# In the last rounds of the token stage, the stores of normed rows and h go ahead of the outputs' stores

## The chip, the core and the metric

The kernel runs on one core of one Trainium2 chip. A core has a matrix engine (TensorE, in the profile PE, its weight loads PEld), VectorE (DVE), ScalarE (ACT), GpSimd (POOL) and SyncE (SP), which here only issues DMAs. Each engine runs its own list of instructions in order and waits on semaphores for the others. The metric is the device time of one execution in microseconds (us).

## The reference

The reference takes x, 8192 tokens (4 sequences of 2048) of 512 numbers, through one transformer layer:

```python
xn = layernorm(x)
cq, ckv = xn @ Wc + bc, xn @ Wckv + bckv
q = [cq @ Wcq + bcq, cq @ Wqr + bqr]      # per token: 16 heads x (32 + 16)
k = [ckv @ Wck + bck, xn @ Wkr + bkr]
v = ckv @ Wv + bv                         # 16 heads x 32
attn = softmax(q k^T / sqrt(48))          # between the heads of one token
x1 = x + layernorm((attn v) @ Wo + bo)
xf = layernorm(x1)
scores = softmax(xf @ gate_w.T)           # 64 experts, the best 6 of each token
routed = sum over them of score * down_e(silu(gate_e(xf)) * up_e(xf))
shared = (silu(xf @ Wsg.T) * (xf @ Wsu.T)) @ Wsd.T
out = x1 + layernorm(routed + shared)
```

The attention runs over the 16 heads of one token, not over tokens. In the reference 16 of each head's 48 numbers of q and k are also turned by an angle of the token's position (rotary embedding). Scores are taken between heads of the same token only, so both sides turn alike and the scores don't change; the kernel leaves the turning out. `h` below is the hidden product silu(gate) * up of the shared part.

## The kernel before

Two programs run one behind the other. The **token stage** (`token_pipeline`) goes over 64 tiles of 128 tokens. The **expert stage** (`experts_and_norm`) gathers each expert's rows from device memory, multiplies, adds them to accumulators in device memory, and then a last pass adds the shared part and norms. Between the two stands a barrier of all engines.

The token stage is a software pipeline. Every engine has a function `iteration(i, par)`; in round i it works on several tiles at once: tile i+1 is normed, i projected, i-1 gets its q, k and v, i-2 its attention, i-3 its output product, i-4 its x1 and second norm, i-5 its gate, up and routing scores, and i-6 is stored. Rounds -2 to 7 and 62 to 69 are unrolled with plain numbers, the rest is a loop over registers. `active(t)` is true in the loop, and for a plain number where 0 <= t < 64.

The attention's output `o` has its heads in the partitions and must be turned into rows of tokens. This goes over device memory: DVE writes `o` in round i-1 (L867, counted by `d_pv`), SP stores it with four DMAs in round i (L368, counted by `o_out`), waits until they have landed, and loads it back with four more as `oin` (L383, `o_in`). PE transposes `oin` (L557) ahead of the second half of the gate and up product and of the product with Wo; in PE's order these come before the transposes of prob and the product of prob with v (L598), which makes the next `o`. The stores' rows in device memory are 128 bytes long.

In the same round SP stores the finished tile i-6: `xf` (L372, 288 KB: normed rows and routing scores, waits for `d_r`, the last DVE instruction of round i-1, L882) and `h` (L375, 192 KB, waits for `d_h`). These stand between the stores of `o` and their reload. `xf` has two buffers; DVE norms tile i-4 into one (L799, in the profile L732 of the helper `normalise`) once the store of tile i-6 has landed (`xf_out`). The order of the DMAs on SP is written out by hand; all of SP's DMAs go through one hardware queue.

At the end of rounds 65 and 66 ScalarE issues the weights of the first four experts (L690 to L694: each time two experts of 768 + 384 KB), right behind its copy of the ranks. In rounds 66 and 67 SP also loads the ranks for the expert stage.

Of the kernel before, what the change touches and what calls it, by code (L numbers as in the profile page):

```python
# [41 lines left out]
NT = T // P  # L42
# [60 lines left out]
def settle(eng):  # L103

    eng.nop(nofuse=True)
# [47 lines left out]
def token_pipeline(nc, x, cst, w_lat, b_lat, w_q, b_q, w_ck, b_ck, w_v, b_v, w_o, b_o, w_gu,  # L153
                   x1_d, xf_d, h_d, acc_d, v_d, o_d, rank_d, wlat, wq, wck, wv, load_expert, c, tri, all_ranks, ranks_in):
    ctx = ExitStack()
    with ctx:
        def sb(name, shape, dt=F32):
            return ctx.enter_context(nc.sbuf_tensor(name, shape, dt))
# [4 lines left out]
        def count(name, per=1, n=1, place=0):  # L163
            return Count(sem(name), per, NT, n, place)
# [41 lines left out]
        xf = sb("xf", [P, 2, D + E])  # L206
        xfT = sb("xfT", [P, 2, KD, P], F32R)
        th = sb("th", [P, SI])
        h = sb("h", [P, 2, SI])
# [56 lines left out]
        h_out = [count(f"h_out{n}", 16, 2, n) for n in range(2)]  # L266
        acc_out = count("acc_out", 32)
        xf_out = [count(f"xf_out{n}", 16, 2, n) for n in range(2)]
# [43 lines left out]
        d_h = count("d_h", 4)  # L312
        d_r = count("d_r", 8)
# [14 lines left out]
        def active(t):  # L328
            return not isinstance(t, int) or 0 <= t < NT

        def pipeline(eng, iteration):
            for i in range(FIRST, LOOP):
                iteration(i, i % 2)
            with eng.Fori(0, PAIRS) as r:
                for u in range(2):
                    iteration(r * 2 + (LOOP + u), (LOOP + u) % 2)
            for i in range(REST, LAST):
                iteration(i, i % 2)

        def rows(ap, t):  # L340
            return ap[t * P:(t + 1) * P, :] if isinstance(t, int) else ap[bass.ts(t, P), :]


        @block.sync
        def _(sp):
            for t in range(2):
                sp.dma_start(xin[:, t, :], rows(x, t)).then_inc(x_in[t].sem, 16)
            sp.dma_start(c[:], cst).then_inc(consts_in, 16)
            for n, (stage, _, _, src) in enumerate(parts):
                if n in SPLIT_BEFORE:  # L350
                    sp.wait_ge(part_lo, SPLIT_BEFORE[n])
                sp.dma_start(stage, src).then_inc(part_in[n], 16)
                if n == KD - 1:
                    sp.dma_start(blat[:], b_lat.partition_broadcast(P)).then_inc(latent_bias_in, 16)

            def load_ranks(a, b):
                sp.dma_start(all_ranks[a:b].rearrange("n e t -> n (e t)"),
                             rank_d[a:b].rearrange("n e t -> n (e t)")).then_inc(ranks_in, 16)

            def iteration(i, par):  # L360
                if active(i - 3):
                    sp.wait_ge(d_pv.sem, d_pv.at(i - 3))
                    sp.wait_ge(o_in.sem, o_in.at(i - 5))
                    dst = o_d[1 - par].rearrange("(c g b) (x d) -> g b x c d", c=8, g=2, b=2, d=DH)
                    src = o[:].rearrange("p (c b d) -> p b c d", c=8, b=2)
                    for g in range(2):
                        for b in range(2):
                            sp.dma_start(dst[g, b], src[64 * g:64 * g + 64, b]).then_inc(o_out.sem, 16)  # L368
                if active(i - 6):
                    sp.wait_ge(d_r.sem, d_r.at(i - 6))  # L370
                    settle(sp)
                    sp.dma_start(rows(xf_d, i - 6), xf[:, par, :]).then_inc(xf_out[par].sem, 16)  # L372
                    sp.wait_ge(d_h.sem, d_h.at(i - 6))
                    settle(sp)
                    sp.dma_start(rows(h_d, i - 6), h[:, par]).then_inc(h_out[par].sem, 16)  # L375
                if active(i - 3):
                    sp.wait_ge(o_out.sem, o_out.at(i - 3))
                    settle(sp)
                    sp.wait_ge(pe_oT.sem, pe_oT.at(i - 4))
                    settle(sp)  # L380
                    src = o_d[1 - par].rearrange("c (h t d) -> t c h d", t=B4, d=DH)
                    for n in range(B4):
                        sp.dma_start(oin[n:P:B4, :].rearrange("p (h d) -> p h d", d=DH), src[n]).then_inc(o_in.sem, 16)  # L383
                if active(i + 2) and (not isinstance(i, int) or i >= 0):

                    sp.wait_ge(d_ln[0].sem, d_ln[0].at(i))
                    settle(sp)
                    sp.dma_start(xin[:, par, :], rows(x, i + 2)).then_inc(x_in[par].sem, 16)
                if isinstance(i, int) and i == FIRST:
                    sp.wait_ge(zeroed, 2)  # L390
                    sp.dma_start(xf_d[T:T + CAP, :], zero[:]).then_inc(scratch_init, 16)
                    for a in acc_d:
                        sp.dma_start(a[T:T + CAP, :], zero[:, 0:D]).then_inc(scratch_init, 16)
                if active(i - 4):
                    sp.wait_ge(g_x1.sem, g_x1.at(i - 4))
                    settle(sp)
                    sp.dma_start(rows(x1_d, i - 4), x1[:]).then_inc(x1_out.sem, 16)
                if active(i - 3):
                    sp.wait_ge(g_x1.sem, g_x1.at(i - 4))
                    settle(sp)  # L400
                    sp.dma_start(xres[:], rows(x, i - 3)).then_inc(xres_in.sem, 16)
                if active(i - 5):
                    for a in acc_d:
                        sp.dma_start(rows(a, i - 5), zero[:, 0:D]).then_inc(acc_out.sem, 16)
                if active(i - 6):
                    sp.wait_ge(a_rank.sem, a_rank.at(i - 6))
                    settle(sp)
                    if isinstance(i, int) and i - 6 >= NT - DIRECT:
                        dst = all_ranks[i - 6:i - 5]
                    else:  # L410
                        dst = rank_d[i - 6] if isinstance(i, int) else rank_d[bass.ds(i - 6, 1)].rearrange("o e t -> (o e) t")
                    sp.dma_start(dst, rank[:, par, :]).then_inc(rank_out[par].sem, 16)
                if isinstance(i, int) and i == 1:
                    sp.wait_ge(zeroed, 3)
                if active(i - 1):
                    sp.wait_ge(d_v.sem, d_v.at(i - 1))
                    sp.wait_ge(v_in[1 - par].sem, v_in[1 - par].at(i - 3))
                    sp.dma_start(v_d[1 - par], v[:]).then_inc(v_out.sem, 16)
                    sp.wait_ge(v_out.sem, v_out.at(i - 1))
                    settle(sp)  # L420
                    sp.wait_ge(pe_pv.sem, pe_pv.at(i - 3))
                    settle(sp)
                    src = v_d[1 - par].rearrange("(cg b t) (j d) -> b (t j) cg d", cg=NBLK, b=2, j=H)
                    for b in range(2):
                        sp.dma_start(vbd[64 * b:64 * b + 64, 1 - par, :, b, :], src[b]).then_inc(v_in[1 - par].sem, 16)
                if isinstance(i, int) and i == NT + 2:
                    for n in range(2):
                        sp.wait_ge(rank_out[n].sem, rank_out[n].at(NT - 18 + n))
                    load_ranks(0, NT - 16)
                if isinstance(i, int) and i == NT + 3:  # L430
                    for n in range(2):
                        sp.wait_ge(rank_out[n].sem, rank_out[n].at(NT - DIRECT - 2 + n))
                    load_ranks(NT - 16, NT - DIRECT)

            pipeline(sp, iteration)
            for n in range(2):
                sp.wait_ge(rank_out[n].sem, rank_out[n].at(NT - 2 + n))
            sp.wait_ge(acc_out.sem, acc_out.at(NT - 1))
            sp.wait_ge(x1_out.sem, x1_out.at(NT - 1))
            for n in range(2):  # L440
                sp.wait_ge(h_out[n].sem, h_out[n].at(NT - 2 + n))
                sp.wait_ge(xf_out[n].sem, xf_out[n].at(NT - 2 + n))
            sp.wait_ge(scratch_init, 48)
# [163 lines left out]
        def _(act):  # L607

            def split(i):

                for n, (stage, w, m, _) in enumerate(parts):
                    if PART_AT[n] == i:
                        act.wait_ge(part_in[n], 16)
                        nc.scalar.copy(w[:, 0, m, :], stage).then_inc(part_hi, 1)
# [799 lines left out]
```

## Time and profile before

| | us |
|---|---|
| median of 3 runs | 1982.51 |
| lowest and highest | 1980.75, 1984.57 |
| profiled execution | 1972.49 |
| its span, first to last instruction | 1970.5 |
| PE busy | 1813.3 (92%) |
| DVE busy | 1482.7 (75%) |
| ACT busy | 1039.2 (53%) |
| POOL busy | 554.7 (28%) |

All times inside the span are microseconds from its start. The token stage ends at about 1357. A row of an engine's order of time gives start, duration, engine (with q where its sequencer issues a DMA), line, operation, destination and source; in brackets stands how long the engine had been idle before it, and what ended this. The names of buffers stand without numbers: `bank` is any of the PSUM banks. A helper's line stands for all its calls.

### The profile page before, as it was taken

Reading aid. Unit: us, or ns where it says so; the run is one execution under the profiler, and the core shown is the slowest. Engines: PE = TensorE matmul, PEld = TensorE weight load, DVE = VectorE, ACT = ScalarE, POOL = GpSimd, SP = SyncE. Lnnn points to the kernel's source line nnn. Section 1 sums busy time; section 2 is a strip of 40 time slices with the busy share of each in tenths; the row PEclk is TensorE's granted clock in tenths of the full one; section 3 lists DMA queues with packets and bytes.
Section 4 is the critical chain, followed back from the end, with each engine's and each line's share of the span. In section 5 each row is a group of like instructions: output and inputs, shape, how many; then the busy total and the mean of one; then the engine's idle time right before and its main releaser. Section 6 shows DMA issues by size and latency. Waiting matters only on the chain. (4 is left out here: it accounts for less than half of the span.)

```text
span 1970.5 us, 49884 instructions
## 1 busy us (share of the span) xinstructions
PE 1813.3 (92%) x14529; PEld 1439.2 (73%) x14529; DVE 1482.7 (75%) x3871; ACT 1039.2 (53%) x2257; POOL 554.7 (28%) x773
## 2 busy tenths in 40 slices
PE   5899999999999999999999999865799999978886
PEld 4788888888888888888888888754455555546564
DVE  6688888888888888888888888854354445439897
ACT  4666666666667676666666666631233333323333
POOL 1112111111212121212121212111344444427777
PEclk8899999999999999999999999987899999989999
DMA  5355656555555555555555555566999999979994
GB/s 194 77 155 132 157 129 158 131 148 142 140 151 141 150 138 153 136 154 136 154 136 153 137 154 133 144 155 202 307 309 312 306 308 310 291 210 398 396 397 163
DMA packets 540056, 384.01 MB, mean 195 GB/s; under 512 B 423848, under 2 KB 432168, under 8 KB 539944
## 3 DMA queue, kind: packets, MB, share of 16 engines
q1 hardware_dynamic: 519456, 324.99, 56.9%
q0 software_dynamic: 14336, 35.66, 7.9%
q10 hardware_dynamic: 6208, 22.68, 3.0%
q8 instruction: 27, 0.44, 0.1%
q14 instruction: 29, 0.24, 0.0%
HBM read 232.46 MB, written 150.63 MB: 194 GB/s over the span
## 5 line engine op out<-in xcount | busy, mean ns | idle before, releaser
L617 ACT COPY kT<-bank 48x256 f32<-48x256 f32 x512 | 309.0, 604 | 12.6
L895 POOL TENSOR_SCALAR ve<-mv 128x1 f32<-128x1 f32 x192 | 42.4, 221 | 959.8 <-DVE mv L728 959.8
L1103 PE MATMUL e_gu<-w,xgT 128*128 128x384 f32 x512 | 187.2, 510 | 13.9 <-issue 12.9
L617 ACT COPY qT<-bank 48x256 f32<-48x256 f32 x512 | 188.1, 367 | 13.3 <-PE bank L453 2.3
L460 PE MATMUL bank<-wgu,xfT 128*128 128x416 f32 x512 | 187.6, 366 | 4.3 <-ACT xfT L617 3.8
L461 PE MATMUL bank<-wgu,xfT 128*128 128x416 f32 x512 | 181.8, 355 | 0.0
L1264 DVE SCALAR_TENSOR_TENSOR tanh<-tanh,e_gu 128x192 f32<-128x192 f32 x64 | 22.6, 354 | 167.9 <-ACT tanh L1190 167.9
L1103 PEld LDWEIGHTS e_gu<-w,xgT 128*128 128x128 f32 x512 | 94.2, 194 | 72.4 <-issue 18.8
L1347 POOL DMA_INDIRECT acc_scratch<-eo,sidx x64 | 101.5, 1586 | 123.7 <-ACT eo L1186 107.5
L1126 PE MATMUL e_ps<-w,hidT 96*128 96x512 f32 x256 | 127.6, 621 | 1.6 <-ACT hidT L1178 0.9
L464 PE MATMUL bank<-wgu,xfT 128*128 128x416 f32 x512 | 119.2, 355 | 0.3 <-DVE xfT L737 0.3
L897 POOL TENSOR_TENSOR rstd<-ve,mhalf 128x1 f32<-128x1 f32 x192 | 114.5, 596 | 16.0
L913 POOL TENSOR_TENSOR x<-yn,xres 128x512 f32<-128x512 f32 x64 | 82.2, 1284 | 116.1 <-DVE yn L732 116.1
L489 PE MATMUL bank<-wlat,xT 128*128 128x512 f32 x256 | 108.2, 423 | 1.4 <-issue 1.4
L746 DVE SCALAR_TENSOR_TENSOR th<-th,bank 128x176 f32<-128x176 f32 (+1 forms) x128 | 44.9, 351 | 85.3 <-ACT th L655 82.3
L1178 ACT COPY hidT<-e_ps 96x256 f32<-96x256 f32 x64 | 23.6, 368 | 159.4 <-PE e_ps L1110 159.4
L1376 POOL TENSOR_TENSOR f_res<-f_acc,f_res 128x512 f32<-128x512 f32 x64 | 95.1, 1508 | 33.5 <-ACT f_acc L1207 17.8
L1207 ACT ACTIVATE f_acc<-f_acc,f_shift,f_rstd 128x512 f32<-128x512 f32 x64 | 48.7, 808 | 105.8 <-POOL f_shift L1368 105.8
L460 PE MATMUL bank<-wo,oT 128*128 128x512 f32 x256 | 102.5, 400 | 1.4 <-ACT oT L617 1.4
L480 PEld LDWEIGHTS score_ps<-kT,qT 48*64 48x64 f32 x4096 | 69.2, 138 | 46.7 <-issue 46.7
L617 ACT CAST oT<-bank 128x512 fp32r<-128x512 f32 x64 | 37.6, 587 | 124.5 <-PE bank L453 124.5
L490 PE MATMUL bank<-wlat,xT 128*128 128x512 f32 x256 | 102.8, 402 | 0.0
(178 smaller groups left out, 4884.8 us busy)
## 6 DMA issues: line engine op xcount, KB each, us to landing
w<-w_eg SPq DMA_DIRECT2D x60, 768.0 KB, 6.0
acc_scratch<-zero SPq DMA_DIRECT2D x130, 256.0 KB, 4.1
w<-w_ed SPq DMA_DIRECT2D x60, 384.0 KB, 7.6
xf_scratch<-xf SPq DMA_DIRECT2D x64, 288.0 KB, 2.1
xin<-x SPq DMA_DIRECT2D x64, 256.0 KB, 3.0
v_scratch<-v SPq DMA_DIRECT2D x64, 256.0 KB, 3.7
vbd<-v_scratch SPq DMA_DIRECT2D x128, 128.0 KB, 3.3
o_scratch<-o SPq DMA_DIRECT2D x256, 64.0 KB, 2.3
```

The lines of the kernel that those rows point to most:

```text
L460: nc.tensor.matmul(dst, a[:, 0], b[:, 0], start=(n == 0), stop=False)
L461: nc.tensor.matmul(dst, a[:, 0], b[:, 1], start=False, stop=False)
L464: last = nc.tensor.matmul(dst, a[:, 1], b[:, 0], start=False, stop=(n == len(lhs) - 1))
L489: nc.tensor.matmul(dst, a[:, 0], b[:, 0], start=(n == 0), stop=False)
L490: nc.tensor.matmul(dst, a[:, 0], b[:, 1], start=False, stop=False)
L617: nc.scalar.copy(dst, src).then_inc(done.sem, 1)
L897: nc.gpsimd.tensor_tensor(rstd[n][:], ve[n][:], mhalf[:], ALU.pow).then_inc(g_rstd[n].sem, 1)
L913: nc.gpsimd.tensor_tensor(x1[:], yn[:], xres[:], ALU.add).then_inc(g_x1.sem, 1)
L1103: last = nc.tensor.matmul(gu_ps[par], xgT[:, par, n, :], w1[:, place, n, :], start=(n == 0), stop=(n == KD - 1))
L1126: last = nc.tensor.matmul(out_ps, hidT[:, n, :], w2[0:PI, (place - 1) % NW, n, :], start=(n == 0), stop=(n == 1))
L1347: nc.gpsimd.indirect_dma_start(acc_d[1 - par], bass.IndirectOffsetOnAxis(sidx[:, (place - 1) % NW, :].bitcast(U32), 0), eo[:, (place - 1) ...
L1376: nc.gpsimd.tensor_tensor(r, acc[:, u, n * D:(n + 1) * D], r, ALU.add).then_inc(g_sum.sem, 1)
```

## The change

SP's stores of `xf` and `h` are put in a function of their own, `store_rows`. In rounds with a plain number i of 64 or more it is called ahead of the stores of `o`; in all others it is called behind them, as before. In rounds 67 to 69 there are no stores of `o`. No other engine's program is changed.

```diff
+            def store_rows(i, par):
+                if active(i - 6):
+                    sp.wait_ge(d_r.sem, d_r.at(i - 6))
+                    settle(sp)
+                    sp.dma_start(rows(xf_d, i - 6), xf[:, par, :]).then_inc(xf_out[par].sem, 16)
+                    sp.wait_ge(d_h.sem, d_h.at(i - 6))
+                    settle(sp)
+                    sp.dma_start(rows(h_d, i - 6), h[:, par]).then_inc(h_out[par].sem, 16)
+
             def iteration(i, par):
+                if isinstance(i, int) and i >= NT:
+                    store_rows(i, par)
                 if active(i - 3):
                     sp.wait_ge(d_pv.sem, d_pv.at(i - 3))
                     sp.wait_ge(o_in.sem, o_in.at(i - 5))
...
                             sp.dma_start(dst[g, b], src[64 * g:64 * g + 64, b]).then_inc(o_out.sem, 16)
-                if active(i - 6):
-                    sp.wait_ge(d_r.sem, d_r.at(i - 6))
-                    settle(sp)
-                    sp.dma_start(rows(xf_d, i - 6), xf[:, par, :]).then_inc(xf_out[par].sem, 16)
-                    sp.wait_ge(d_h.sem, d_h.at(i - 6))
-                    settle(sp)
-                    sp.dma_start(rows(h_d, i - 6), h[:, par]).then_inc(h_out[par].sem, 16)
+                if not isinstance(i, int) or i < NT:
+                    store_rows(i, par)
                 if active(i - 3):
                     sp.wait_ge(o_out.sem, o_out.at(i - 3))
```

## Rows read from the trace of the kernel before

**Rows 1.** the page's share of busy time: engine, busy us (share), instructions.
```profile
...
PE 1813.3 (92%) x14529; PEld 1439.2 (73%) x14529; DVE 1482.7 (75%) x3871; ACT 1039.2 (53%) x2257; POOL 554.7 (28%) x773
...
```

**Rows 2.** rounds as windows: us, engines' busy us (instructions), clock, DMA, GB/s.
```profile
...
1246.46:1266.58 20.12, 19.67 (x198) 17.21 (x196) 17.00 (x41) 13.22 (x30) 2.84 (x5) 1.00 0.50 131
1266.58:1286.18 19.60, 15.63 (x173) 13.83 (x173) 15.43 (x37) 11.52 (x27) 2.82 (x5) 1.00 0.52 135
...
1306.94:1333.80 26.86, 13.37 (x53) 11.31 (x53) 10.14 (x26) 3.01 (x8) 4.11 (x6) 0.73 0.87 229
...
```

**Rows 3.** SP's order of time, 1262 to 1330: start us, us, instruction.
```profile
...
1266.58 2.63 SPq L368 DMA_DIRECT2D o_scratch<-o  x4
1269.30 0.57 SPq L372 DMA_DIRECT2D xf_scratch<-xf  x1
...
1270.87 3.58 SPq L383 DMA_DIRECT2D oin<-o_scratch  x4
...
1286.18 2.63 SPq L368 DMA_DIRECT2D o_scratch<-o  x4
...
1290.47 2.58 SPq L383 DMA_DIRECT2D oin<-o_scratch  x4
...
1306.94 4.34 SPq L368 DMA_DIRECT2D o_scratch<-o  x4
1311.38 3.18 SPq L372 DMA_DIRECT2D xf_scratch<-xf  x1
1314.65 0.38 SPq L375 DMA_DIRECT2D h_scratch<-h  x1
1316.35 2.59 SPq L383 DMA_DIRECT2D oin<-o_scratch  x4
...
```

**Rows 4.** VectorE's order of time, the same stretch, idle time before in brackets.
```profile
...
1265.87 0.68 DVE L867 TENSOR_TENSOR o<-bank,srec 128x512 f32<-128x512 f32 x1
...
1267.11 1.29 DVE L882 TENSOR_SCALAR xf<-ex,erec 128x64 f32<-128x64 f32 x1
...
1294.93 0.34 DVE L746 SCALAR_TENSOR_TENSOR th<-th,bank 128x176 f32<-128x176 f32 x1 [3.09 <-ACT th L655]
...
1322.71 0.69 DVE L737 TENSOR_TENSOR oT<-bank,oT 128x512 fp32r<-128x512 f32 x1 [4.60 <-ACT oT L617]
...
```

**Rows 5.** PE's order of time, the same stretch.
```profile
...
1276.65 0.66 PE L453 MATMUL bank<-c,oin 128*128 128x128 f32 x4 [0.96 <-DMA oin<-o_scratch]
...
1294.70 1.51 PE L480 MATMUL score_ps<-kT,qT 48*64 48x64 f32 x64 [2.45 <-ACT kT L617]
1296.14 1.11 PE L453 MATMUL bank<-c,oin 128*128 128x128 f32 x4
...
1320.93 1.12 PE L453 MATMUL bank<-c,oin 128*128 128x128 f32 x4 [10.48 <-DMA oin<-o_scratch]
...
```

**Rows 6.** VectorE's waits, 1262 to 1330: us in total, times, longest.
```profile
...
DVE xf L732 <- DMA xf_scratch<-xf: 10.6, 3, 6.6
...
```

**Rows 7.** ScalarE's order of time, last issue of the first weights.
```profile
...
1306.44 0.62 ACTq L137 DMA_DIRECT2D w<-w_ed  x1
```

**Rows 8.** DMAs in narrow stretches: issues with us to landing, and the fetch.
```profile
...
q8 instruction: 1, 0.02, 48.8%
...
oin<-o_scratch SPq DMA_DIRECT2D x1, 64.0 KB, 2.5
...
h_scratch<-h SPq DMA_DIRECT2D x1, 192.0 KB, 2.7
...
w<-w_ed ACTq DMA_DIRECT2D x1, 384.0 KB, 8.4
...
xf_scratch<-xf SPq DMA_DIRECT2D x1, 288.0 KB, 6.6
```

**Rows 9.** PE's clock around its gaps, windows as in group 2.
```profile
...
1296.90:1298.74 1.84, 1.84 (x7) 1.77 (x6) 1.70 (x6) 0.59 (x1) 0.00 (x0) 0.50 0.68 247
...
1320.93:1326.01 5.08, 5.08 (x17) 4.89 (x17) 1.57 (x7) 0.59 (x1) 0.00 (x0) 0.50 1.08 260
...
```

## The prediction, made before the changed kernel ran

> **What bounds the kernel now.** I read the page first, then the tail of the token stage by rounds, then each engine's order of time there. On the page TensorE is busy for 92% of the span [rows 1], but that average is made by the steady loop. A steady round of 20.12 us holds 19.67 us of PE; the round that begins with token tile 63's output store, 26.86 us long, holds 13.37 [rows 2]. The change acts in three rounds only: i = 64, 65 and 66, where the outputs of tiles 61, 62 and 63 are stored. Rounds 67 to 69 have no outputs' stores, so nothing is reordered there. In the three rounds PE is no longer full; what does it wait for?
>
> It waits for two things: ScalarE's copies of kT (2.45 us in round 65) and the reload of the outputs, `oin`: 0.96 us in round 64, none in round 65, where the transposes of `oin` follow the scores directly, and 10.48 us in round 66 [rows 5]. So the chain "DVE writes `o`, SP stores it, waits for the landing, SP loads it back, PE transposes it" already ends last in rounds 64 and 66, and in 65 it has a small slack. Everything that PE does later in a round (gate and up product, output product, transposes of prob, the product with v) follows those transposes on one in-order engine, and the next `o` follows them. A late `oin` therefore delays the next round whole.
>
> VectorE also shows waits, for the landing of the normed rows (L732, 10.6 us in three places) [rows 6]. These are what the change shortens. They don't set the end: in round 65 the next instruction waits 3.09 us more, for ScalarE's tanh, and in round 66 VectorE is idle again for 4.60 us before L737, which needs `oin` [rows 4].
>
> **Part 1: the new wait on SP.** Before, SP issues the four outputs' stores as soon as `o` is written (d_pv). In round 64 that is 1265.87 + 0.68 = 1266.55, and the issue stands at 1266.58. Afterwards SP first waits for d_r, which counts the last VectorE instruction of the previous round, L882: 1267.11 + 1.29 = 1268.40 [rows 3, 4]. That is 1.85 us later. The same pair recurs in the two other rounds, with 1.8 to 1.9 us between its ends. The wait on d_h costs nothing, since h is written before `o`. Queued behind the waiting SP instruction are the outputs' stores, their reload, the x1 and xres transfers and the zero stores; of these only the reload has no room.
>
> **Part 2: two issues ahead of the stores.** The xf store takes SP 0.57 us and the h store 0.38, and between two issues lies about 0.1 (1266.58 + 2.63 = 1269.21, next at 1269.30): 1.1 us together, estimated [rows 3]. So the outputs' stores begin 1.85 + 1.10 = 2.95 us later in each of the three rounds. Before, these 1.1 us lay under the landing of the fourth output store (reload issued at 1270.87), where they were free. The cover is lost: after the fourth store SP will only wait.
>
> **Round 64.** The chain is late already, so all 2.95 us count, if nothing else in it changes. One thing may: an instruction fetch of some 16 KB (0.02 MB) starts on a DMA engine between 1270.4 and 1270.6 [rows 8], and the reload's four issues took 3.58 us there against 2.58 in round 65 [rows 3]. If the fetch then falls outside the longer chain, the cost is about 1.1 less, 1.8. At 1270.5 SP will be in the middle of the four stores, so I let it hit them: **+2.9** (ends 1.8 and 3.0).
>
> **Round 65.** The reload was issued from 1290.47 for 2.58 us; its fourth transfer begins at about 1292.4 and lands 2.5 us later, at 1294.9 [rows 3, 8]. PE took it at 1296.14 [rows 5], a slack of 1.2. Cost 2.95 - 1.24 = **+1.7** (ends 1.5 and 1.9).
>
> **Round 66.** Here expert weights are on the wires: 2.36 MB issued by ScalarE until 1307.06, the last landing 1306.44 + 8.4 = 1314.8 [rows 7, 8]. The outputs' stores, issued from 1306.94, back up (4.34 us of issue instead of 2.63, then 3.18 for xf), and the reload starts only at 1316.35, 1.5 us after the weights [rows 3]. So most of the 2.95 us is hidden, as the stores have to wait for the weights anyway. What isn't hidden is the order in the ring: now the 480 KB of xf and h pass first. Before, both landed behind the outputs, and trailed them by 1.1 us: h, issued at 1314.65, took 2.7 us, to 1317.35, while the outputs were in by about 1316.25, just ahead of the reload [rows 3, 8]. Swapped, the outputs are the ones that trail. I take **+1.1**. At best the order doesn't matter and the cost is 0; at worst the fourth output store cannot be issued before the ring drains, and its 2.5 us to landing come on top of the weights' end: +2.5.
>
> The Trainium skill, "DMA: Bandwidth & Descriptors", section "Queues, rings and completion order", says that one ring's descriptors are consumed in order, and that an engine takes turns between the queues that have work. By the turns the outputs' stores would get through beside the weights, round 66 would pay the whole shift of 2.95, and the sum below would be 1.85 more. This trace speaks against it for such a burst: the stores issued at 1306.94 weren't through before the weights, and an xf store issued at 1333.88 behind the second burst took 6.6 us to land [rows 8].
>
> **Clock.** PE's clock falls after idle stretches. In round 65, behind the gap of 2.45 us, it was granted 0.50 in 1296.90 to 1298.74; behind the gap of 10.48 us it stayed at 0.50 for 5.08 us of work (1.2 instead of 2.4 GHz); round 64 with its single gap of 0.96 for `oin` kept 1.00 throughout [rows 2, 9]. With the change the gap in round 64 becomes 0.96 + 2.9 = 3.9 us, longer than the one that brought it down in round 65. I take 1.3 us lost there (2.5 us of work at half rate; ends 0 and 2.5, the latter from 5.08 us at half rate). In round 65, already down, the extra 1.7 us of idling may keep it down longer: +0.5 (0 to 1.7). Round 66 is down in both: 0.
>
> **Sum.** 2.9 + 1.7 + 1.1 + 1.3 + 0.5 = **+7.5 us**. On the profiled execution (1972.49 us, span 1970.5) this makes 1980.0. The median of the runs shown is 1982.51, 10 us above that execution; the shift is the same, so 1990.0. All low ends: 1.8 + 1.5 + 0 + 0 + 0 = 3.3 (1985.8). All high ends: 3.0 + 1.9 + 2.5 + 2.5 + 1.7 = 11.6 (1994.1). After round 66 each step hangs on the one before, so nothing gives the time back: the second burst of weights is itself issued behind round 66's rank copy and moves along.
>
> **Rivals.**
> - *Almost hidden* (chance 0.17): the fetch falls outside, the clock holds, the ring order costs nothing. About +3.5, 1986.0, near the edge of what can be told. For it: the gap in round 64 is a single one, and round 66 is bound by the weights. Against it: the two wait terms alone make 3.3.
> - *Faster, because VectorE's waits are the bound* (0.09): xf's landing moves forward by 0.9 us in rounds 64 and 65 (issue right after d_r instead of 1269.30, and clear of the fetch, so up to the whole 2.2 us wait in 64) and by about 1.7 in round 66. If those waits ended last the gain would be 2.2 + 0.9 + 1.7 = 4.8 us, 1977.7. It decides from the point at which `oin` has over 3 us of slack in each round; the rows show 0, 1.2 and 0.
> - *The clock stays down* (0.12): PE idles enough in both rounds to be at 1.2 GHz through most of 64 and 65; 10 to 12 us, 1994.
> - *It doesn't act*: the condition asks for a plain number i of at least 64, and rounds 62 to 69 are unrolled with plain numbers. It acts; under 0.02.
>
> **How the numbers follow.** The forecast itself has 0.60. A measurement of this kernel can't tell less than 0.2%, 4 us, from no change (the three runs span 3.8). Above 1986.5 lie the forecast, the clock case and a little of the hidden one: slower 0.74. Same 0.17, faster 0.09. Range: 1983.5 to 1994.5, which takes in all ends of the terms and the hidden case with the spread of the runs, and leaves out the faster one.
>
> **What would show it.** In the trace after: SP's order in the three rounds xf, h, then the four stores, these beginning 2.9 us after `o` instead of 0.03; PE idle for `oin` about 3.9 us in round 64, 1.7 in 65 and 11 to 12 in 66; VectorE's waits for xf shorter with no step of PE earlier; a granted clock of 0.50 somewhere in round 64; the token stage ending 6 to 9 us later, the expert stage as long as before. I am wrong if `oin` lands no later relative to `o`, if PE's waits for it don't grow, or if round 66 shrinks because its stores leave the weights' burst behind.

## The result: 0.39% slower, and the profile after

| | before | changed |
|---|---|---|
| median of 20 runs, us | 1984.09 | 1990.59 |
| ratio to before, 95% interval | | 1.0039 [1.0023, 1.0056] |
| profiled execution: span, us | 1970.5 | 1981.5 |

On the median of before that is +7.7 us, with an interval of 4.6 to 11.1 (the two medians themselves differ by 6.5). The forecast was +7.5. The single pair of profiles differs by 11.0 us of span; what follows shows why that is more than the timed difference.

The code of the changed kernel stands 6 lines lower on the other engines. SP's order of time in the changed kernel, which answers to [rows 3]:

```profile
...
1270.48 0.33 SPq L364 DMA_DIRECT2D xf_scratch<-xf  x1
...
1271.38 3.32 SPq L379 DMA_DIRECT2D o_scratch<-o  x4
1276.34 2.58 SPq L389 DMA_DIRECT2D oin<-o_scratch  x4
...
1296.22 2.67 SPq L379 DMA_DIRECT2D o_scratch<-o  x4
1300.54 2.58 SPq L389 DMA_DIRECT2D oin<-o_scratch  x4
...
1320.72 3.78 SPq L379 DMA_DIRECT2D o_scratch<-o  x4
1328.39 2.59 SPq L389 DMA_DIRECT2D oin<-o_scratch  x4
...
```

Its VectorE's order of time, for [rows 4]:

```profile
...
1267.88 0.68 DVE L873 TENSOR_TENSOR o<-bank,srec 128x512 f32<-128x512 f32 x1
...
1269.12 1.28 DVE L888 TENSOR_SCALAR xf<-ex,erec 128x64 f32<-128x64 f32 x1
...
1302.14 0.34 DVE L752 SCALAR_TENSOR_TENSOR th<-th,bank 128x176 f32<-128x176 f32 x1 [3.70 <-ACT th L661]
...
1334.81 0.69 DVE L743 TENSOR_TENSOR oT<-bank,oT 128x512 fp32r<-128x512 f32 x1 [7.29 <-ACT oT L623]
```

Its PE's order of time, for [rows 5]:

```profile
...
1281.36 1.11 PE L459 MATMUL bank<-c,oin 128*128 128x128 f32 x4 [3.62 <-DMA oin<-o_scratch]
...
1301.91 1.16 PE L486 MATMUL score_ps<-kT,qT 48*64 48x64 f32 x64 [2.43 <-ACT kT L623]
1306.44 1.12 PE L459 MATMUL bank<-c,oin 128*128 128x128 f32 x4 [3.37 <-DMA oin<-o_scratch]
...
1333.04 1.11 PE L459 MATMUL bank<-c,oin 128*128 128x128 f32 x4 [11.62 <-DMA oin<-o_scratch]
...
```

The steps read off one by one. SP now begins with xf, behind the routing scores (1269.12 + 1.28 = 1270.40), and the outputs' stores start at 1271.38, 3.50 us behind the start of `o` instead of 0.71. In round 65 it is 1292.70 to 1296.22, 3.52, in round 66 3.53: later by 2.8 each, where 2.95 was forecast. PE's idle time for `oin` went from 0.96, 0 and 10.48 us to 3.62, 3.37 and 11.62. In round 66 VectorE's wait ahead of the `oT` add, which needs `oin`, grew (7.29 at 1334.81, 4.60 before): what it gains at xf it loses at `oin`.

To read the rounds I cut the stretch at the starts of VectorE's write of `o` (tiles 61, 62, 63), at PE's transposes of `oin`, and at VectorE's first copy behind the barrier (line 1235 before, 1241 changed), the start of the expert stage. The first cut goes into "to transposes" and "transposes to next o". All entries are differences of starts in the orders of time, us, taken before rounding, so that some are off by 0.01 from the rows shown.

| profile | order in 64, 65, 66 | 64: to transposes, then to o | 65: the same | 66: to transposes | then to the barrier |
|---|---|---|---|---|---|
| before | old, old, old | 10.78, 8.82 | 10.67, 10.09 | 14.71 | 36.84 |
| changed | new, new, new | 13.48, 11.34 | 13.74, 10.76 | 15.85 | 37.05 |

These two profiles alone give +2.7, +2.5, +3.1, +0.7, +1.1 and +0.2, together 10.3. The other 0.7 us of the spans lie outside the stretch: +2.0 ahead of it and -1.3 behind.

Clock in the changed kernel, in the same form as [rows 9]:

```profile
...
1282.12:1286.74 4.62, 4.62 (x15) 4.42 (x14) 1.57 (x7) 0.66 (x2) 0.00 (x0) 0.50 0.54 200
1307.20:1310.64 3.44, 3.44 (x12) 3.29 (x11) 1.58 (x7) 0.58 (x1) 0.00 (x0) 0.50 0.14 48
...
```

Round 64 now has 4.62 us of PE's work at 0.50, where before the round had none.

### The profile page after: what moved, and what is told of

Read it like the earlier page. It is cut to its first block and busy times, and to the rows that moved or that the text cites. A ratio compares the mean times of both kernels' runs of the same rounds, so it can differ in the third digit from the quotient of the medians.

```text
span 1981.5 us, 49884 instructions
## 1 busy us (share of the span) xinstructions
PE 1819.0 (92%) x14529; PEld 1443.7 (73%) x14529; DVE 1483.2 (75%) x3871; ACT 1037.9 (52%) x2257; POOL 554.3 (28%) x773
## 5 line engine op out<-in xcount | busy, mean ns | idle before, releaser
L623 ACT COPY qT<-bank 48x256 f32<-48x256 f32 x512 | 187.7, 367 | 13.7 <-PE bank L459 2.6
L466 PEld LDWEIGHTS bank<-wgu,xfT 128*128 128x128 f32 x512 | 99.0, 193 | 6.3 <-ACT xfT L623 4.9
```

Of the source, the lines that this page charges most:

```text
L466: nc.tensor.matmul(dst, a[:, 0], b[:, 0], start=(n == 0), stop=False)
L623: nc.scalar.copy(dst, src).then_inc(done.sem, 1)
```

## Experiments

All were kernels of this same program. Single profiles, unless a ratio is given.

**The changed kernel again.** No edit.

> The changed kernel once more, to see which of its terms repeat. Stretches are counted between the starts of VectorE's writes of o: round 64 took 19.60 us before and 24.82 changed, round 65 20.76 and 24.49, and from o of tile 63 to the first instruction behind the barrier 51.55 and 52.90. If the late issue and the clock are the cause, 24 to 25.5, 23 to 25 and 52 to 54 again. If the 1.4 us that round 65 cost above the forecast is an accident of where an instruction fetch fell, its reload (5.90 us from first issue to PE's transposes) comes back at 4.5 to 5.0 here; if the fetch is bound to the program's progress, 5.5 to 6.2 again.

```profile
...
1282.72 1.12 PE L459 MATMUL bank<-c,oin 128*128 128x128 f32 x4 [4.01 <-DMA oin<-o_scratch]
...
1307.31 1.12 PE L459 MATMUL bank<-c,oin 128*128 128x128 f32 x4 [3.43 <-DMA oin<-o_scratch]
...
1334.02 1.12 PE L459 MATMUL bank<-c,oin 128*128 128x128 f32 x4 [11.99 <-DMA oin<-o_scratch]
...
```

Round 64 took 24.73 us, round 65 24.29, and 16.22 + 36.83 = 53.05 the rest. The terms repeat. Round 65's reload took 5.97 us from its first issue to the transposes: not an accident.

**One round at a time.**

```diff
-                if isinstance(i, int) and i >= NT:
+                if isinstance(i, int) and i == NT + 0:
                     store_rows(i, par)
...
-                if not isinstance(i, int) or i < NT:
+                if not isinstance(i, int) or i != NT + 0:
                     store_rows(i, par)
```

The other two kernels have NT + 1 and NT + 2 in both places.

> The new order in round 64 alone. Theory (each round pays for its own late stores): round 64 24 to 25.5 us, round 65 20.3 to 21.3 and the rest 51 to 52.5, as before. Rival (the first round disturbs the clock and the phases of what follows, and the later rounds' cost comes from that): rounds 65 and the rest also longer, by 2 us or more together.

> The new order in round 65 alone. Theory: round 64 19.3 to 20 us; round 65 longer by 2 to 4.5 us, 23 to 25, of which 1.7 is the 2.95 us of later issue less the slack of 1.24, and the rest is the instruction fetch that the later reload runs into and the clock; the rest 51 to 52.5. Rival: without the disturbance of round 64 it pays 1.7 or less.

> The new order in round 66 alone. Theory (the stores wait for the burst of expert weights anyway; what costs is that xf and h pass ahead in the ring): rounds 64 and 65 as before (19.6, 20.8); from o of tile 63 to PE's transposes of oin 15.5 to 16.2 us against 14.71, the rest of the token stage 36.5 to 37.5 behind them. Rival (the burst gives no cover, or the taking of turns between queues holds): 17 us or more.

| new order in | round 64 | round 65 | 66: to transposes | to the barrier |
|---|---|---|---|---|
| 64 alone | 24.44 | 20.77 | 14.75 | 32.70 |
| 65 alone | 23.57 | 24.45 | 14.92 | 37.83 |
| 66 alone | 20.69 | 20.66 | 15.53 | 36.10 |

Each round pays for its own order, and nearly the same with or without the others: 24.4, 24.4 and 15.5, against 24.8, 24.5 and 15.9 with all three. The rival of a knock-on falls. What nobody expected stands in the first column: with the *old* order round 64 took 23.57 and 20.69, not 19.60. And in "64 alone" the last stretch was 3 to 5 us shorter than in the other kernels with the old order in round 66 and the late weights (35.5 to 37.8); that stays unexplained, it was seen once.

In "65 alone" the fourth reload transfer is seen by itself, and a fetch of instructions that starts while it is under way:

```profile
...
oin<-o_scratch SPq DMA_DIRECT2D x1, 64.0 KB, 3.6
```

```profile
...
q8 instruction: 1, 0.02, 27.5%
...
```

It took 3.6 us to land, against 2.5 in the kernel before [rows 8], and a 16 KB instruction fetch starts in 1307.3 to 1307.5, 11.3 us behind the start of `o`. In the profile before, the reload had landed by then.

**The kernel before again.** No edit.

> The kernel before once more. Round 64 in the old order took 19.60 us in the first profile, but 20.69 and 23.57 in the two kernels that keep the old order there; the stores' landing took 6.1 us in both instead of 4.3. If a fetch of instructions falls by chance on the stores or behind them, round 64 takes anything from 19.6 to 23.6 here, and the other stretches repeat: 20.8 for round 65, 14.7 to the transposes in round 66. If those kernels' changed orders were the cause, 19.6 comes back.

```profile
...
1271.63 2.63 SPq L368 DMA_DIRECT2D o_scratch<-o  x4
...
1277.86 2.58 SPq L383 DMA_DIRECT2D oin<-o_scratch  x4
...
```

```profile
...
1270.92:1293.84 22.92, 17.34 (x175) 15.25 (x174) 15.80 (x37) 12.15 (x27) 3.03 (x6) 0.93 0.45 115
...
1283.44:1286.82 3.38, 3.38 (x12) 3.26 (x13) 2.28 (x9) 0.59 (x1) 0.00 (x0) 0.50 0.79 298
...
```

```profile
...
q8 instruction: 1, 0.02, 15.0%
...
```

Round 64 took 22.92 us in the unchanged kernel. The reload starts 6.23 us after the stores, not 4.29; the fetch starts in 1275.0 to 1275.4, 4.1 to 4.5 us behind the start of `o`, against 4.5 to 4.7 in the first profile [rows 8]. PE's work behind the transposes runs at 0.50 for 3.38 us. So the profile before caught a lucky round 64. Round 65 repeats (20.66), round 66 nearly (15.14), the end too (37.16).

**The wait alone.** The order of the DMAs stays old:

```diff
             def iteration(i, par):
+                if isinstance(i, int) and NT <= i < NT + 3:
+                    sp.wait_ge(d_r.sem, d_r.at(i - 6))
+                    settle(sp)
                 if active(i - 3):
```

> The old order of the DMAs, but in rounds 64 to 66 SP waits for the routing scores (d_r) ahead of the outputs' stores: the new wait without the two issues and 480 KB in front. Theory (late issue): stores 2.5 us behind the start of o instead of 0.7; round 65 21.4 to 22.8 us (1.85 less the slack of 1.24, with or without the fetch), round 64 1 to 3 us longer than in the old order, round 66 14.6 to 15.2 to the transposes, since the weights hide it. Rival (what costs is the bytes of xf and h ahead in the ring): rounds 64 and 65 as in the old order within 0.5, since nothing stands in front of the stores.

```profile
...
1304.78 1.12 PE L456 MATMUL bank<-c,oin 128*128 128x128 f32 x4 [1.69 <-DMA oin<-o_scratch]
...
1330.67 1.11 PE L456 MATMUL bank<-c,oin 128*128 128x128 f32 x4 [10.64 <-DMA oin<-o_scratch]
...
```

The stores start 2.67 us behind the start of `o`. Round 65 took 23.21 us, 2.5 more than the old order, somewhat above the range I gave: 1.6 to the transposes and 0.9 of clock behind them. Round 64 took 23.19, inside the old order's own spread, so one profile shows nothing there. Round 66 took 1330.67 - 1315.79 = 14.88 to the transposes, nothing more than the old order: there the weights hide a start 1.95 us later.

**The store of h alone ahead.**

```diff
             def iteration(i, par):
+                if isinstance(i, int) and i >= NT:
+                    store_h(i, par)
                 if active(i - 3):
                     sp.wait_ge(d_pv.sem, d_pv.at(i - 3))
...
                     sp.dma_start(rows(xf_d, i - 6), xf[:, par, :]).then_inc(xf_out[par].sem, 16)
-                    sp.wait_ge(d_h.sem, d_h.at(i - 6))
-                    settle(sp)
-                    sp.dma_start(rows(h_d, i - 6), h[:, par]).then_inc(h_out[par].sem, 16)
+                if not isinstance(i, int) or i < NT:
+                    store_h(i, par)
```

> In rounds 64 to 69 the store of h alone goes ahead of the outputs' stores; xf stays behind them, so there is no new wait: one issue and 192 KB in front. Late issue: stores 1.2 us behind the start of o, round 65 20.7 to 21.2 us (inside the slack of 1.24), and in round 66 0.4 to 0.6 more to the transposes (15.1 to 15.4), because h passes ahead behind the weights. Rival (ring order costs nothing): round 66 14.7.

```profile
...
1285.21 0.72 SPq L364 DMA_DIRECT2D h_scratch<-h  x1
1290.44 2.63 SPq L376 DMA_DIRECT2D o_scratch<-o  x4
...
1305.97 0.33 SPq L364 DMA_DIRECT2D h_scratch<-h  x1
1311.16 4.55 SPq L376 DMA_DIRECT2D o_scratch<-o  x4
...
```

I had the issue wrong: h was ready early and SP idle, so the store went out at 1285.21, 4.5 us ahead of `o` (1289.72), and the outputs' stores still start 0.72 us behind it. It cost nothing: round 65 20.72, round 66 14.99 to the transposes, inside the old order's 14.7 to 15.1. As its bytes had left before the burst began, this says nothing on the ring order.

**The scores ahead of o.** The changed order, and VectorE's two instructions of L886 and L888, now in a function `gate_rows`, moved ahead of L873 in rounds 63 to 65:

```diff
+                if isinstance(i, int) and NT - 1 <= i < NT + 2:
+                    gate_rows(i, par)
                 if active(i - 2):
                     dve.wait_ge(pe_pv.sem, pe_pv.at(i - 2))
...
-                if active(i - 5):
-                    dve.wait_ge(a_gate.sem, a_gate.at(i - 5))
...
+                if not isinstance(i, int) or not NT - 1 <= i < NT + 2:
+                    gate_rows(i, par)
```

> The changed order, but in rounds 63 to 65 VectorE writes the routing scores (the two instructions that d_r waits for) ahead of o, so that the wait is over when o is. Late issue: stores 1.8 us behind the start of o instead of 3.5; round 65 20.8 to 22.5 us instead of 24.4, round 64 1.5 to 2.5 less than 24.7, round 66 still 15.6 to 16.2 to the transposes, as there the order counts and not the wait. Rival (the 480 KB in front are the cost): rounds 64 and 65 stay at 24 to 25.

> The changed order with VectorE's routing scores ahead of o in rounds 63 to 65, now timed. If the wait for the scores and the issues behind it are the cost in rounds 64 and 65, and the ring order costs 1 us in round 66, it is 6 to 7 us faster than the changed kernel: within 0.15% of the kernel before. If the 480 KB in front are the cost, it stays 0.3 to 0.4% slower than the kernel before.

```profile
...
1286.65 0.34 SPq L364 DMA_DIRECT2D xf_scratch<-xf  x1
1287.09 1.36 SPq L367 DMA_DIRECT2D h_scratch<-h  x1
1288.54 2.77 SPq L379 DMA_DIRECT2D o_scratch<-o  x4
...
1307.06 0.33 SPq L364 DMA_DIRECT2D xf_scratch<-xf  x1
1307.49 0.39 SPq L367 DMA_DIRECT2D h_scratch<-h  x1
1308.19 5.91 SPq L379 DMA_DIRECT2D o_scratch<-o  x4
1318.51 2.59 SPq L389 DMA_DIRECT2D oin<-o_scratch  x4
...
```

The first profile: rounds 64 and 65 19.52 and 20.69 us, as in the old order, though the same 480 KB still go in front. In round 65 the stores start 1.75 us behind `o`. In round 66 xf and h go out while VectorE waits for PE, the stores start 0.72 us behind `o` (1307.47), no later than in the old order, and still the transposes come 15.82 us behind it, against 14.7 to 15.1: here nothing but the order in the ring is left. The second profile gave 23.75, 19.45 and 15.73; in its round 66 the stores start 1.31 us behind `o`. Timed, the ratio to before was 1.0006 [0.9980, 1.0032]. That is as expected, but it doesn't settle it alone: the interval reaches into that of the changed kernel (from 1.0023), and the two were not timed side by side. What carries the reading is rounds 64 and 65 of the first profile and round 65 of the second. In that second profile's round 64 the reload follows 6.15 us behind the stores, as in the slow rounds of the old order, with a fetch 5.0 us behind `o`; in the first profile of the same kernel the fetch came only 10.3 us behind `o`, and it took 4.30.

**Two experts' weights earlier.** Old order; the block that issues the weights moves from the end of ScalarE's rounds 65 and 66 to behind its copy of `oin`:

```diff
                     copy(oT[:, 0].rearrange("p k t -> p (k t)"), b3, a_oT)
+                if isinstance(i, int) and 0 <= i - NT - 1 < 2:
+                    act.wait_ge(pe_k.sem, pe_k.at(NT - 1))
+                    settle(act)
+                    for e in range(2):
+                        load_expert(act, 2 * (i - NT - 1) + e, 2 * (i - NT - 1) + e)
...
-                if isinstance(i, int) and 0 <= i - NT - 1 < 2:
-                    act.wait_ge(pe_k.sem, pe_k.at(NT - 1))
-                    settle(act)
-                    for e in range(2):
-                        load_expert(act, 2 * (i - NT - 1) + e, 2 * (i - NT - 1) + e)
```

> The old order of stores; ScalarE issues the two bursts of expert weights behind its copy of oin in rounds 65 and 66 instead of behind the copy of the ranks, so the first burst (some 9.7 us) fits between round 65's reload and round 66's stores. Theory (in round 66 the outputs' stores wait for the burst): from o of tile 63 to PE's transposes 10.4 to 11.5 us instead of 14.9, and less of the clock lost behind; the second burst is over before xf of tile 61 is stored, which took 6.6 us to land. Token stage 6 to 11 us shorter, in time 0.3 to 0.55% faster. Rival (the bursts only move to where they do the same harm): no difference, within 2 us.

The same with the changed order:

> The changed order with the same early bursts. Theory: without the burst round 66 pays for the later stores in full, as round 65 does: 13.2 to 14.2 us to the transposes, 3 us more than with the old order and early bursts (with the late bursts it is 1.0 more); in all 8 to 11 us slower than that kernel, about as fast as the kernel before. Rival (round 66's 1.0 was the whole price of the ring order and nothing was hidden): 1.0 to 1.5 us more in round 66.

SP's rows in round 66 of the kernel with the old order:

```profile
...
1306.69 3.00 SPq L368 DMA_DIRECT2D o_scratch<-o  x4
...
1312.51 2.59 SPq L383 DMA_DIRECT2D oin<-o_scratch  x4
...
```

PE's transposes in round 66 of the kernel with the changed order:

```profile
...
1325.26 1.11 PE L459 MATMUL bank<-c,oin 128*128 128x128 f32 x4 [8.36 <-DMA oin<-o_scratch]
...
```

Old order: 11.31 us to the transposes, 3.6 less than before, as expected, but the rest still took 36.83. That the second burst only moved to where it hurts as much fits this, and isn't shown. The time was 0.9992 [0.9967, 1.0017] of before: the gain of 0.3 to 0.55% that I expected didn't show. Changed order: 12.58 to the transposes, 1.3 more than its partner, not the 3 I had expected. The reason is in SP's rows: the partner's stores start at 1306.69, 6.2 us behind the last issue of the burst (until 1300.47), back up (3.00 us of issue instead of 2.63), and their reload begins 5.82 us later; the changed order's stores start later, clear of it, and need 4.33. So the pair is not the clean test that I meant. The time was 1.0023 [1.0001, 1.0045] of before, and the median 5.6 us above its partner's, under the 8 to 11 expected.

**One expert's weights at a time.** Old order; `load_expert(act, i - NT - 1, i - NT - 1)` behind the copy of `oin` in rounds 65 and 66 and behind the copy of the ranks in rounds 67 and 68.

> The old order of stores; one expert's weights (1.15 MB) at a time instead of two: behind the copy of oin in rounds 65 and 66, and behind the copy of the ranks in rounds 67 and 68. Theory: each piece is over before the next transfer that somebody waits for; from o of tile 63 to PE's transposes 10.0 to 10.8 us (14.9 before, 11.3 with two experts at a time, whose end still met the stores), and from there to the end of the token stage 33 to 36 instead of 36.8, since xf of tile 61 lands sooner. Token stage 5 to 9 us shorter, 0.25 to 0.45% faster. Rival (the late weights then hold up the first experts, or the time falls to the clock): within 0.15% of the kernel before.

```profile
...
1318.92 1.12 PE L453 MATMUL bank<-c,oin 128*128 128x128 f32 x4 [5.29 <-DMA oin<-o_scratch]
...
```

```profile
...
1309.65 2.65 SPq L368 DMA_DIRECT2D o_scratch<-o  x4
...
1313.96 2.59 SPq L383 DMA_DIRECT2D oin<-o_scratch  x4
...
```

The transposes come 9.99 us behind `o` (1308.93), the reload 4.31 behind the stores, as in an undisturbed round, and 35.53 us remain. The time is 0.9956 [0.9931, 0.9981] of before, faster than the kernel before, and so than the changed one, which was the slower of the two. PE's idle time for `oin` is 5.29 us instead of 10.48: about half of that wait was the weights' burst, which the change left where it was; the other half stays without it. It also gives a size of what the burst hides: in the kernel with the changed order and early bursts, where the stores are clear of the weights too (4.33 us to the reload), the same stretch took 12.58, so later stores cost 2.6 us when nothing covers them and 1.0 when the burst does. This rests on one profile of each, and the two differ also in where the weights stand.

## Why the forecast was right, step by step

With the profiles that keep the late bursts, each term has three or four values in either order (old: the two profiles of before and the single-round kernels; new: changed, again, and the single-round kernels):

| term | forecast | old order, mean (range) | new order, mean (range) | measured |
|---|---|---|---|---|
| 64: to transposes | +2.9 | 11.8 (10.8 to 12.5) | 13.6 (13.3 to 13.9) | +1.8 |
| 64: transposes to next `o` (clock) | +1.3 | 9.9 (8.8 to 11.4) | 11.1 (10.8 to 11.3) | +1.2 |
| 65: to transposes | +1.7 | 10.6 (10.3 to 10.9) | 13.7 (13.5 to 13.8) | +3.1 |
| 65: transposes to next `o` (clock) | +0.5 | 10.1 (9.8 to 10.4) | 10.7 (10.5 to 11.0) | +0.6 |
| 66: to transposes | +1.1 | 14.9 (14.7 to 15.1) | 15.9 (15.5 to 16.2) | +1.0 |
| sum | +7.5 | | | +7.7 |

The single values of a row lie up to 2.6 us apart, so the differences are good to about 1 us, an estimate; the timed +7.7 has its own interval. The stretch behind round 66's transposes is left out (36.1 us on average in the old order, with the odd 32.70, and 36.7 in the new).

- **The new wait and the two issues (2.95 us in each round).** Right: 2.8 us. The wait alone makes 1.95 of it, and in round 65 1.6 of the 3.1 us to the transposes. The two issues cost the rest only because they stand behind the wait: with the scores ahead of `o` they mostly slip into SP's idle time, and round 65 in both profiles and round 64 in the first lose nothing, which the forecast had not seen.
- **Round 64, mis-sized upwards.** The step "I let it hit them" took the fetch to be in the chain in both orders and the base to be 19.6. The repeats show that the old order meets the same fetch in two ways: at 4.6 us behind `o` it delays only the reload, at 4.1 to 4.3 the stores too, and then the round is 1 to 4 us longer. The fetch is not all of it: with the fetch at 4.6 and the clock down behind the transposes (two experts' weights earlier) the round took 22.61. The new order pays in all four of its profiles. The difference of the means is my low end for this term, 1.8.
- **Round 65, mis-sized downwards.** "2.95 less the slack of 1.24" assumed that the reload, moved back by 2.9 us, would take as long as before. It moved onto the next fetch, and its fourth transfer took 3.6 us instead of 2.5. 1.7 + 1.1 and a little is the 3.1 measured, above my high end of 1.9. That the fetch is the cause is inferred from its time, not shown by moving it.
- The two errors, -1.1 and +1.4, cancel: that the sum fits to 0.2 us is luck; its sign and its size of several us are not.
- **Round 66 and the weights' cover.** Right in size and in mechanism. The wait alone cost nothing there, the order alone 0.9 (15.82 against 14.9), both together 1.0. In the changed kernel, xf is issued 2.4 us behind the last weights and lands 6.5 us later, 1326.3, just behind those weights (1317.41 + 8.5 = 1325.9):

```profile
...
w<-w_ed ACTq DMA_DIRECT2D x1, 384.0 KB, 8.5
```

```profile
...
xf_scratch<-xf SPq DMA_DIRECT2D x1, 288.0 KB, 6.5
```

  In the kernel before, only 13 packets of the outputs' stores, out of 2048, started between their first issue at 1306.94 and 1312.00, beside 352 packets of weights. The Trainium skill's rule of turns between queues ("DMA: Bandwidth & Descriptors", "Queues, rings and completion order") would have let xf and the outputs pass beside the weights. The traces don't show that; for a burst like this one the measurement decides.
- **The clock.** Right in size, but the step "longer than the one that brought it down" is too simple, and in the old order too round 64 often loses it: four of six profiles had 10.4 us or more behind the transposes. A lucky profile hid that. Over all 14 profiles of this document the stretch took 8.8 to 9.0 us in the three in which the clock stayed at 1.00 (before, 66 alone, the first with the scores ahead of `o`) and 10.2 to 11.6 in the others. It fell behind all eight gaps for `oin` of 2.10 us or more, but also behind three of six shorter ones: behind 0.30 (the store of h ahead), 1.19 and 1.45, and not behind 0.96, 1.05 and 1.69. So round 64 lost the clock in all four profiles of the new order, as it did in some of the old.
- **VectorE's waits for xf** became shorter, by 1.8 and 1.5 us in rounds 64 and 66 (in round 65 none is left), and bought nothing: the next instruction waits for ScalarE or `oin`. The faster rival falls.
- **Nothing given back later.** Right: from round 66's transposes to the barrier 35 to 38 us in either order, but for the one 32.70.

## What to carry to other kernels

In a round trip over memory (store, wait for landing, reload) the place behind the stores was free here for other issues. The place ahead of them was free only where the other stores had nothing left to wait for when `o` was due; behind a wait, or with a burst on the wires, it cost. So look at what the moved step waits for before its bytes. Before a wait is shortened, look whether the instruction behind it would wait anyway, and for whom: here half of the long wait belonged to a burst of prefetches, and issuing that burst earlier and one expert at a time gave the 0.44% that reordering the stores could not (earlier alone, in whole bursts, gave nothing that could be told). And take a round's length from more than one profile before an effect of a few microseconds is read from it.

## What the runs showed of the hardware that was not expected

- An instruction fetch of 16 KB in unrolled code goes with 1 to 2 us on a chain of small DMAs, and where it strikes depends on a few tenths of a microsecond: in round 64 of the old order stores to reload took 4.29 us with the fetch about 4.6 us behind `o` (two kernels), and 6.02 to 6.23 with it 4.1 to 4.3 us behind (four profiles). The two profiles of the kernel with the scores ahead of `o` agree: 4.30 us with the fetch 10.3 behind `o`, 6.15 with it 5.0 behind. That the fetch is the cause is read from this agreement; it was not tried by moving it. Its time alone doesn't decide, since in that last case it came 3.93 us behind the first store's issue, and in the kernel before, where the reload followed after 4.29, at 3.91.
- A gap on PE can have a second price, and whether it has differs between executions of one kernel. In the kernel before, run again, a gap of 2.60 us ahead of round 64's transposes was followed by a granted clock of 0.50 in 1283.44 to 1286.82, and the stretch behind took 10.40 us instead of 8.82, behind a gap of 0.96.
- In this kernel's burst of 2.36 MB a smaller store that was issued later got nearly nothing until the last part of the burst (6.5 us to landing for xf in the changed kernel, 2.4 in round 65 of the kernel before, which has no burst).

```profile
...
xf_scratch<-xf SPq DMA_DIRECT2D x1, 288.0 KB, 2.4
```
